# Means ahead of the squared deviations, variances on GpSimd, a split wait of the gate, shared PSUM banks and new orders in a 512-token layer kernel

## The reference

```python
v = x @ W_write.T
# W_t = gamma * W_{t-1} + v_t x_{t-1}^T, scanned in chunks of 64 tokens
reads = W_t-weighted sums of v over earlier tokens      # causal, decayed
x1 = layernorm(x + x + alpha * (reads @ W_read.T))
q(a)  = blockwise FP4 (blocks of 16): a / scale to the grid 0, .5, 1, 1.5, 2, 3, 4, 6
gate, up = q(x1) @ q(w_gate).T, q(x1) @ q(w_up).T       # 704 wide
h   = silu(gate) * up
out = layernorm(x1 + q(h) @ q(w_down).T)
```

## Time and profile before

| | |
|---|---|
| median of 3 runs | 324.37 us (324.2 to 324.91) |
| span of the profiled execution | 322.5 us |
| PE busy | 314.5 us (97%) |
| VectorE busy | 293.0 us (91%) |
| ScalarE busy | 213.2 us (66%) |
| GpSimd busy | 238.2 us (74%) |

### The profile page before, as it was taken

The page is one execution under the profiler, slowest core; times in us unless marked ns, Lnnn a source line. Parts: engine busy times, 40 slices in busy tenths (PEclk is TensorE's granted clock), DMA queues, the critical chain, the costliest instruction groups (busy, mean ns, idle before and its releaser), DMA issues.

```text
span 322.5 us, 6519 instructions
## 1 busy us (share of the span) xinstructions
PE 314.5 (97%) x2067; PEld 285.2 (88%) x2067; DVE 293.0 (91%) x746; ACT 213.2 (66%) x521; POOL 238.2 (74%) x258
## 2 busy tenths in 40 slices
PE   7999999999999999999999999999999999999994
PEld 3999988989998998999989998898989889998983
DVE  4799789989899999899998999889999999999973
ACT  7769994767775647844784556766675555665664
POOL 1999898668696868676886768777779588368872
PEclk9999999999999999999999999999999999999999
DMA  6830301010010200320020200021000000001002
GB/s 227 302 125 9 132 0 67 1 66 2 1 67 16 84 16 0 100 82 3 16 83 17 83 17 3 33 65 35 1 18 17 16 18 17 19 16 35 17 33 84
DMA packets 8242, 15.69 MB, mean 49 GB/s; under 512 B 1040, under 2 KB 5136, under 8 KB 8208
## 3 DMA queue, kind: packets, MB, share of 16 engines
q1 hardware_dynamic: 7920, 15.01, 14.0%
q10 hardware_dynamic: 288, 0.26, 0.3%
HBM read 11.08 MB, written 4.19 MB: 47 GB/s over the span
## 4 chain that ended last, share of the span: by engine, by line
PE 69%; DVE 17%; issue 5%; ACT 4%; POOL 3%; ACTq 0%; DVEq 0%; POOLq 0%
PE gu L1712 11%; PE gu L1716 11%; PE gu L1713 11%; PE bank L1817 5%; PE bank L1712 4%; PE bank L1716 4%; PE bank L1713 4%; PE bank L1722 3%; DVE h_y L1094 3%; PE bank L1725 3%; PE bank L1726 3%; DVE w_raw L1209 2%; DVE hqT_lo L1236 2%; DVE h_am L1215 2%; PE bank L1783 2%
## 5 line engine op out<-in xcount | busy, mean ns | idle before, releaser
L413 POOL TENSOR_TENSOR h_q<-h_g,h_ns 128x704 f32<-128x704 f32 x32 | 51.2, 1604 | 47.7 <-DVE h_g L1099 47.6
L1712 PE MATMUL gu<-guT_hi,xqT_hi 128*128 128x512 f32 (+1 forms) x192 | 74.0, 386 | 0.7 <-DVE w_raw L1209 0.6
L1713 PE MATMUL gu<-guT_lo,xqT_hi 128*128 128x512 f32 (+1 forms) x192 | 72.2, 376 | 0.0
L1716 PE MATMUL gu<-guT_hi,xqT_lo 128*128 128x512 f32 (+1 forms) x192 | 56.6, 376 | 0.0
L699 ACT ACTIVATE w_raw<-gu 128x512 f32<-128x512 f32 x64 | 29.3, 462 | 32.7 <-PE gu L1716 32.4
L406 POOL TENSOR_TENSOR h_n<-w_raw,h_rs 128x704 f32<-128x704 f32 x32 | 47.0, 1472 | 3.4 <-DVE h_rs L1089 3.2
L719 ACT CAST hqT_hi<-bank 128x512 fp32r<-128x512 f32 x64 | 30.4, 478 | 17.7 <-PE bank L1817 17.2
L1712 PEld LDWEIGHTS gu<-guT_hi,xqT_hi 128*128 128x128 f32 x192 | 36.1, 188 | 6.0 <-ACT xqT_hi L688 0.9
L1716 PEld LDWEIGHTS gu<-guT_hi,xqT_lo 128*128 128x128 f32 x192 | 35.5, 188 | 6.0 <-ACT xqT_lo L693 0.2
L1713 PEld LDWEIGHTS gu<-guT_lo,xqT_hi 128*128 128x128 f32 x192 | 36.1, 188 | 4.8
L1094 DVE SCALAR_TENSOR_TENSOR h_y<-h_sq,h_n 128x704 f32<-128x704 bf16 x34 | 36.9, 1090 | 0.0
(11 more groups left out here) (159 smaller groups left out, 936.7 us busy)
## 6 DMA issues: line engine op xcount, KB each, us to landing
xs<-in_x_rows_dram SPq DMA_DIRECT2D x8, 512.0 KB, 3.4
out_dram<-wq_gu SPq DMA_DIRECT2D x32, 128.0 KB, 1.7
x_full<-in_xt_rows_dram SPq DMA_DIRECT2D x7, 512.0 KB, 3.2
w_raw<-in_w_ffn_dram SPq DMA_DIRECT2D x6, 352.0 KB, 6.0
...
scal<-in_scalars_dram ACTq DMA_DIRECT2D x1, 1.0 KB, 1.7
```

What stands on the lines that cost most here:

```text
L413: nc.gpsimd.tensor_tensor(blocks(h_q[:, p, 0:I]), blocks(h_g[:, p, :]), per_block(h_ns[:, p, :], HB), ALU.mult).then_inc(h_quant, 1)
L1712: nc.tensor.matmul(dst, lh, rh, start=(first and i == 0), stop=False)
L1713: nc.tensor.matmul(dst, lh, rl, start=False, stop=False)
L1716: last = nc.tensor.matmul(dst, ll, rh, start=False, stop=(end and i == len(terms) - 1))
```

## The change

The row means are formed on VectorE right after the residual (`x_mean`, two instructions of one column, and `out_mean`, one), and the squares on ScalarE take the negated mean as bias. The variance is a new instruction on GpSimd, in `x_stats` and `out_stats`, which wait for the squares and then for their own variance.

```diff
-            def x_rstd(n, u):
+            def x_stats(n, u):
 
                 c = slice(2 * u, 2 * u + 2)
-                pool.wait_ge(z_var, 2 * n + u + 1)
+                pool.wait_ge(z_dev, 2 * n + u + 1)
                 if n > 0:
                     pool.wait_ge(x1_ready, 2 * n + u - 1)
+                nc.gpsimd.tensor_scalar(z_ve[:, c], z_ssq[:, c], 1.0 / D, LN_EPS, ALU.mult, ALU.add).then_inc(z_var, 1)
+                pool.wait_ge(z_var, 2 * n + u + 1)
                 nc.gpsimd.tensor_tensor(z_rstd[:, c], z_ve[:, c], neg_half[:], ALU.pow).then_inc(z_rstd_ready, 1)
                 pool.wait_ge(z_rstd_ready, 2 * n + u + 1)
                 nc.gpsimd.tensor_tensor(z_shift[:, c], z_nm[:, c], z_rstd[:, c], ALU.mult).then_inc(z_shift_ready, 1)
...
+            def out_stats(k, p):
 
                 c = slice(p, p + 1)
+                pool.wait_ge(o_dev, k + 1)
+                if k >= 2:
+                    pool.wait_ge(out_ready, k - 1)
+                nc.gpsimd.tensor_scalar(o_ve[:, c], o_ssq[:, c], 1.0 / D, LN_EPS, ALU.mult, ALU.add).then_inc(o_var, 1)
                 pool.wait_ge(o_var, k + 1)
                 nc.gpsimd.tensor_tensor(o_rstd[:, c], o_ve[:, c], neg_half[:, 0:1], ALU.pow).then_inc(o_rstd_ready, 1)
+                if k == LAST * TILES + TILES - 1:
+                    return
                 pool.wait_ge(o_rstd_ready, k + 1)
                 nc.gpsimd.tensor_tensor(o_shift[:, c], o_nm[:, c], o_rstd[:, c], ALU.mult).then_inc(o_shift_ready, 1)
...
 
-                act.wait_ge(z_ready, 2 * n + u + 1)
+                act.wait_ge(z_mean, 2 * n + u + 1)
                 z = x1[:, n % XBUF, :, :]
                 for i in (2 * u, 2 * u + 1):
-                    last = nc.scalar.activation(z_off[:, i, :], z[:, i, :], ACT.Square, bias=z_sum[:, i:i + 1],
-                                                scale=-float(D), accum_out=z_ssq[:, i:i + 1])
+                    last = nc.scalar.activation(z_off[:, i, :], z[:, i, :], ACT.Square, bias=z_nm[:, i:i + 1],
+                                                scale=1.0, accum_out=z_ssq[:, i:i + 1])
                 last.then_inc(z_dev, 1)
...
-            def x_moments(n, u):
-
-                c = slice(2 * u, 2 * u + 2)
-                dve.wait_ge(z_dev, 2 * n + u + 1)
-                if n > 0:
-                    dve.wait_ge(z_shift_ready, 2 * n + u - 1)
-                nc.vector.tensor_scalar(z_nm[:, c], z_sum[:, c], -1.0 / D, None, ALU.mult)
-                nc.vector.tensor_scalar(z_ve[:, c], z_ssq[:, c], 1.0 / D ** 3, LN_EPS, ALU.mult,
-                                        ALU.add).then_inc(z_var, 1)
+            def x_mean(n, u):
+
+                dve.wait_ge(z_ready, 2 * n + u + 1)
+                for i in (2 * u, 2 * u + 1):
+                    last = nc.vector.tensor_scalar(z_nm[:, i:i + 1], z_sum[:, i:i + 1], -1.0 / D, None, ALU.mult)
+                last.then_inc(z_mean, 1)
...
-            def out_moments(k, p):
+            def out_mean(k, p):
                 c = slice(p, p + 1)
-                dve.wait_ge(o_dev, k + 1)
-                nc.vector.tensor_scalar(o_nm[:, c], o_sum[:, c], -1.0 / D, None, ALU.mult)
-                nc.vector.tensor_scalar(o_ve[:, c], o_ssq[:, c], 1.0 / D ** 3, LN_EPS, ALU.mult,
-                                        ALU.add).then_inc(o_var, 1)
+                if k >= 2:
+                    dve.wait_ge(o_shift_ready, k - 1)
+                dve.wait_ge(o_ready, k + 1)
+                nc.vector.tensor_scalar(o_nm[:, c], o_sum[:, c], -1.0 / D, None, ALU.mult).then_inc(o_mean, 1)
```

```diff
 
-            def gate_up(k, b, t, half):
+            def gate_up(k, b, t, half, free=()):
                 fresh = t % 2 == 0 and half == 0
                 if fresh:
                     pe.wait_ge(xqT_hi_ready, 2 * b + t // 2 + 1)
                 if k >= 1:
-                    pe.wait_ge(h_ready, 2 * k + half - 1)
+                    pe.wait_ge(h_ready if half else silu_ready, 2 * k + half - 1)
                 c = slice(t * P, (t + 1) * P)
+                wait_all(free)
                 for m in range(2 - half):
+                    if k >= 1 and m == 1:
+                        pe.wait_ge(h_ready, 2 * k - 1)
                     w = slice(1024, 2 * I) if half else slice(512 * m, 512 * m + 512)
-                    last = split_matmuls(gu[:, 2, 0:2 * LEFT] if half else gu[:, m, :],
```

PSUM is one tensor of eight banks. Banks 0 to 2 stay with gate and up; each single use of the other five takes its bank from a table, so r_at[1] gives reads(1,0) and reads(1,1) the same bank 4:

```diff
-        v_bank, xq_bank = (bank[2], bank[1]), (bank[1], bank[3])
-        s_bank, r_bank = (gu[:, 3, :], bank[0], bank[3], gu[:, 3, :]), (bank[2], bank[1])
...
+        r_at = ((6, 4),
+                (4, 4),
+                (5, 5),
```

All five queues are written in new orders, without a repeated body. The table shows only a line or two of it here:

```diff
+            reads(1, 0, [(wT_lo_ready, 4)])
+            reads(1, 1, [(z_ready, 3)])
```

2081 lines of the change are left out of this document (1217 added, 864 removed), and 3 rows, old and new, of the table h_at.

## The result

The changed kernel takes **359.24 us** (359.15 to 360.68), against 324.34 us for the kernel before beside it: the ratio is 1.108, 95% interval 1.106 to 1.111. It is 34.9 us slower, where 3.1 us were forecast. The profiled span is 357.6 us.

A forecast was written before the change was run, and what follows sets the result against it. PE was taken as the bound, standing still for only 5.6 us; 324.4 + 4.2 (head) - 1.3 (after the head) + 0.2 (tail) = 327.5 us, with an 8 in 10 range of 323.2 to 329.8.

The forecast's parts named there:

- What bounds the kernel before: Whole span: PE is the bound and stands still only 5.6 us, 1.8 in the head and 3.8 after it.
- The head: Up to gate_up(0,0): waits on PE grow from 1.8 to 6.0 us, +4.2, first gate product at 49.7.
- the bank: Head: reads(1,1) shares the bank of reads(1,0) and waits until x_residual(1,0) has read it; 1.05 us lost.
- After the head: After gate_up(0,0): gate's split wait, free banks and less VectorE work take 1.3 of 3.8 us of waits away.
- VectorE (-8 us of busy time): Whole span: one-column means replace x_moments and out_moments, saving up to 11 us of 293 busy; 8 counted.
- GpSimd (+13, 251): Whole span: 48 small instructions at 0.27 us add 13 us (7 to 37), busy time 238 to 251.
- the 0.4 that the forecast had named as its sign of falling: Variances on GpSimd: the forecast falls if they cost 0.4 us or more each; 0.19 was taken.
- The batch stage: Between gate_up(15) and gate_up(17): GpSimd has 40.7 us of work beside 45 us of matmuls, 90% busy.
- The gate's wait: After the head: the gate product waits for silu alone, some 0.7 us earlier, removing few waits; part of -1.3.
- Tail: End of the program: mean ahead of the squares, variance on GpSimd ahead of the power; +0.2 us, 0 to 0.4.
- Rival D: Head: the waits add up rather than hide, +5.4, giving 328.7 us; 8 in 100.
- Rival C: Batch stage: waits between GpSimd and VectorE make PE wait 2 us more than forecast, 329.5 us; 12 in 100.

The follow-up runs named there:

- a_bank: The changed kernel with reads(1,1) in bank 7 alone, behind pr_ready 10 in place of z_ready 3: 359.15 us.
- The halved steps: GpSimd's h_normalise and h_dequant and VectorE's h_magic_add and h_to_grid on half their columns: 339.67 us in the changed kernel, 321.47 in the kernel before.
- b_moments: The kernel before with the statistics' change alone (early means on VectorE, 48 variances on GpSimd), old order, banks and gate: 331.54 us.
- b_vdve: The kernel before with the means ahead of the squares on VectorE, the variances left on VectorE where they stood: 329.0 us.
- b_gate: The kernel before with the gate's split wait alone, the gate product waiting for silu only: 324.28 us.

## Why the prediction was wrong, point by point

**What bounds the kernel before** was right: 5.6 us of waits on PE, and nearly everything measured is a change of those (34.4 of 34.9 us). That the clock would stay at its full level in the new kernel was taken over from the earlier trace rows without a word; it is 2.9 of the 34.4.

**The head (+4.2).** The direction and five places were right: 0.6 ahead of v_subtract(0,1), 0.7 (0.85 forecast) ahead of w_subtract(0), 0.4 ahead of w_subtract(4), 0.35 ahead of reads(1,0), and the bank. Others were not: values(1,0) and values(2,0) lose 0.15 and 0.11, and values(3,0), which was to wait 1.6 us for GpSimd's remainders, starts right behind xq_subtract; 0.6 and 0.7 us are lost ahead of it, at the second xq_transpose and xq_subtract. The bank's wait was 2.2 in place of 1.05, since the step ahead of the residual on VectorE was not in the term. The gate product stood at 51.9 for 49.7, outside the bounds of 48.2 to 50.9. What fell is the reading of the terms as repairs of their own: a_bank shows that a wait taken away comes back in the next steps.

**After the head (-1.3).** This is the step that failed, by 29 us: -1.3 was forecast, and the waits went from 3.8 to 31.7 us, +27.9. The forecast walked single chains, from a product on PE through the other engines to its use, at the durations of the old trace, and asked whether the matmuls in between cover them. It left out what stands ahead in each engine's queue. Counted in matmul work from the two orders and the pitch of the earlier trace rows, reads(n,u) to the xq_transpose of the same n, u was 43.6 us apart in the mean before and 25.4 after; gate_up(k) to h_transpose(k) 26.2 and 22.6. This shrinking of the margin was there to be counted ahead of the run, and it was not: with the old margins a late step was absorbed, with the new ones it can pass on. The halved steps speak for it (19.6 us come back, against 2.8 in the kernel before). But the mean margin does not tell where the loss falls. By the same count it shrinks from 30 to 16 us for gate_up(12) to gate_up(15), ahead of the largest loss; for tiles 20 to 23 it is 24 us in both kernels and for tiles 24 to 27 it grows from 23 to 25, and PE still loses 2.5 (1.6 of it by the clock) and 2.9 us more there than before. So the margins are a part of the cause and argued rather than shown; what each queue had standing ahead of the late step is the other part, and was followed for single waits only.

**VectorE (-8 us of busy time).** Wrong: 293.0 to 295.1, and 293.0 in b_moments. The 552 ns of z_nm were named a wait for GpSimd, and then counted as saved. In b_vdve they are at z_ve, the next small instruction in line, and in b_moments most of them at x_g and x_y.

**GpSimd (+13, 251).** 250.3 in the old order, so the sum was right there (the shortest variance is 0.19, as taken); 257.3 in the new one, where they are held up by VectorE: a variance is 0.36 to 0.39 us there, just under the 0.4 that the forecast had named as its sign of falling. The batch stage, at 90% by the forecast, came to 34.3 us busy of 46.0 (75%, from 168 to 214 us), and PE waited 8.4 us on the way from tile 12 to tile 16: GpSimd didn't fill, it waited in turns.

**The gate's wait** was put among the gains after the head. It is worth nothing in the old order (b_gate) and up to 3.9 us in the new one, much of that by the clock.

**Tail (+0.2).** From the start of the last matmul to the end of the span it is 5.0 us before and 5.6 after. The variance and power of the last tile in the changed kernel answer to the earlier trace rows:

```profile
352.83 0.15 DVE L1406 TENSOR_SCALAR o_nm<-o_sum 128x1 f32<-128x1 f32 x1
353.02 0.51 ACT L784 ACTIVATE o_off<-wq_gu,o_nm 128x256 bf16<-128x256 f32 x1 [1.05 <-DVE o_nm L1406]
...
353.71 0.19 POOL L435 TENSOR_SCALAR o_ve<-o_ssq 128x1 f32<-128x1 f32 x1 [0.57 <-ACT o_off L784]
353.98 0.54 POOL L437 TENSOR_TENSOR o_rstd<-o_ve,neg_half 128x1 f32<-128x1 f32 x1
```

Between the last matmul and the power it is 2.00 us (351.98 to 353.98) against 1.75: +0.25, as forecast. The rest of the 0.6 is behind the issue of the last store (355.06 to the end of the span, 2.5 us, against 2.2 from 320.36). But the same 0.2 to 0.3 us stand in the chain of residual, mean and squares of every tile whose squares wait for the sum, and that was counted only for the last one. In the old order the early means are worth 4.7 us (b_vdve). This step was missing from the sum.

**The rivals.** Rival D, the waits in the head adding up to +5.4, is nearest to the head's +6.5. Rival C had a right mechanism, the two engines holding each other up, and gave it 2 us in one stage. In the new order it is outside that stage too (the loss followed above), and it works through dependent small instructions more than through busy time: taking the variances away gives 7.5 us. No rival had 20 us or more after the head. The Trainium skill's rule in "Perfetto Trace Analysis", section "Optimizing Scalar/DVE Operations", that moving work between these two engines might not help, agrees with b_moments against b_vdve: 48 small instructions are moved, and 2.5 us are lost.

The sum of the 34.9 us as the runs split it, to 0.2 us: 4.7 the mean ahead of the squares, 2.5 the variances on GpSimd, 0 the gate, 27.9 orders and banks together with what they make of the statistics, of the gate and of the clock. How much of the 27.9 is banks and how much is order stays open: apart from one bank (a_bank, nothing) no run changes the one without the other.
